# Linear attention stage of a three-stage kernel: norm gain and bias folded into the weights, the key minimum as the exponential's bias, an fp32 query product, and keys times values split by sequence

## The reference

```
x  = x + attention(ln(x)*(1+scale1)+shift1) @ proj * gamma1
x  = x + gelu((ln(x)*(1+scale2)+shift2) @ fc1 + b1) @ fc2 * gamma2       (b2 inside)
xn = ln(x) * norm_g + norm_b
q, k, v = xn @ Wq + bq, xn @ Wk + bk, xn @ Wv + bv        16 heads of 16
q  = softmax over the 16 channels of a head
k  = softmax over the 64 tokens of a sequence
ctx = k^T v by head;  y = q ctx
h  = silu(ln(y)*sn_g*(1+scale) + (sn_b*(1+scale) + shift)) @ out_W + out_b
x  = x + cond * h
```

## Time and profile before

| | us |
|---|---|
| median of 3 runs | 1348.47 |
| profiled execution | 1349.81 |
| its span | 1347.9 |
| busy PE, DVE, ACT, POOL | 1152.5, 994.8, 867.3, 933.9 |

### The profile page before, as it was taken

The page is one execution under the profiler, slowest core; times in us unless marked ns, Lnnn a source line. Parts: engine busy times, 40 slices in busy tenths (PEclk is TensorE's granted clock), DMA queues, the critical chain, the costliest instruction groups (busy, mean ns, idle before and its releaser), DMA issues. The chain is left out here.

```text
span 1347.9 us, 38178 instructions
## 1 busy us (share of the span) xinstructions
PE 1152.5 (86%) x12189; PEld 856.6 (64%) x12342; DVE 994.8 (74%) x2388; ACT 867.3 (64%) x2268; POOL 933.9 (69%) x1091
## 2 busy tenths in 40 slices
PE   2568898998989874899999999978888888888886
PEld 1356777777777763466666666655666666666664
DVE  2857787887878754745556465439999999999993
ACT  1456677777777762545454544528888888888884
POOL 3547677777777755656575765635788888888888
PEclk9789999999999997899999999989999999999997
DMA  5454233232333332110101001000011111111112
GB/s 149 152 112 117 56 52 62 54 60 56 57 61 53 65 54 66 40 32 16 32 16 31 18 29 32 17 16 7 24 37 51 35 35 50 36 37 36 52 36 71
DMA packets 142704, 67.73 MB, mean 50 GB/s; under 512 B 80688, under 2 KB 141360, under 8 KB 142640
## 3 DMA queue, kind: packets, MB, share of 16 engines
q1 hardware_dynamic: 109472, 40.53, 14.2%
q10 hardware_dynamic: 33168, 26.38, 6.9%
HBM read 41.18 MB, written 8.65 MB: 37 GB/s over the span
## 5 line engine op out<-in xcount | busy, mean ns | idle before, releaser
L1107 PE MATMUL f_ps_y<-w_fc,f_h_split 128*128 128x256 bf16 x1536 | 172.7, 273 | 1.4 <-DVE f_branch L1213 1.4
L1134 PE MATMUL f_ps_h<-f_x_split,w_fc 128*128 128x512 bf16 x737 | 165.8, 381 | 3.1 <-DVE f_x_split L1187 1.5
L1107 PEld LDWEIGHTS f_ps_y<-w_fc,f_h_split 128*128 128x128 bf16 x1536 | 150.2, 98 | 22.5 <-issue 1.7
L627 POOL TENSOR_TENSOR e_split<-e_full,e_split 128x1024 bf16<-128x1024 f32 x64 | 136.6, 2135 | 32.7 <-ACT e_full L700 31.6
L1221 DVE TENSOR_TENSOR f_h_split<-f_h,f_h_split 128x512 bf16<-128x512 f32 x64 | 65.0, 1018 | 103.0 <-ACT f_h L1091 103.0
L1090 ACT ACTIVATE f_h_split<-f_ps_h,b_fc 128x512 bf16<-128x512 f32 x128 | 89.0, 695 | 66.0 <-POOL f_h_split L1045 32.6
L1134 PEld LDWEIGHTS f_ps_h<-f_x_split,w_fc 128*128 128x128 bf16 x768 | 75.4, 98 | 87.0 <-issue 2.2
L609 POOL TENSOR_TENSOR x_split<-x_t,x_split 128x256 bf16<-128x256 f32 x64 | 44.6, 697 | 104.4 <-ACT x_split L649 104.4
L760 PE MATMUL ps_s<-qk_t,k_pairs 128*128 128x64 bf16 x3072 | 101.7, 194 | 11.7 <-DMA k_pairs<-qk_t 9.8
L760 PEld LDWEIGHTS ps_s<-qk_t,k_pairs 128*128 128x128 bf16 x3072 | 99.0, 99 | 14.5 <-DMA k_pairs<-qk_t 11.0
L1045 POOL TENSOR_TENSOR f_h_split<-f_h,f_h_split 128x512 bf16<-128x512 f32 x64 | 80.6, 1269 | 36.3 <-ACT f_h L1091 36.3
(11 more groups left out here) (171 smaller groups left out, 3416.1 us busy)
## 6 DMA issues: line engine op xcount, KB each, us to landing
v_pairs<-v_split SPq DMA_DIRECT2D x128, 66.0 KB, 2.1
k_pairs<-qk_t SPq DMA_DIRECT2D x256, 32.0 KB, 2.2
gain<-gammas SPq DMA_DIRECT2D x64, 128.0 KB, 3.0
f_gain<-gammas ACTq DMA_DIRECT2D x32, 256.0 KB, 4.3
l_gate<-in_cond ACTq DMA_DIRECT2D x128, 64.0 KB, 2.6
out<-x_all ACTq DMA_DIRECT2D x16, 512.0 KB, 2.9
x_all<-in_x SPq DMA_DIRECT2D x13, 512.0 KB, 6.5
w_ada<-in_L_cond_ada_w SPq DMA_DIRECT2D x1, 1536.0 KB, 8.3
```

The costliest lines, as they stand in the source:

```text
L627: pool.tensor_tensor(flat(e_split[a][:, LO]), flat(e_full[:]), flat(e_split[a][:, HI]), ALU.subtract).then_inc(e_lo_made, 1)
L1107: last = pe.matmul(ps_y[:, i], h_split[a][:, hs, f, i * P:(i + 1) * P], m.w_fc2[:, ws, f], start=(f == 0 and k == 0), stop=(f == F_CHUNKS ...
L1134: last = pe.matmul(ps_h[f % 4][:], m.w_fc1[:, ws, c, f * P:(f + 1) * P], x2_split[a][:, xs, c], start=(k == 0 and c == 0), stop=(k == 2 an ...
```

## The change

In the linear pass:

- The affine (L1480) is gone. norm_g is multiplied into the weights when they are split, norm_b times the weights is added to the biases. x3_high and x3_low read the transposed x from PSUM.
- The keys' weights and bias are negated. The minimum of the negated keys (with their bias in PSUM, two more matmuls in qkv) is used as bias of an exponential with scale -1. k_top_bias and k_shifts are gone.
- kq_high is split into k_high (bf16) and q_copy (fp32); kq_low becomes k_low, for the keys alone. kv_high and kv_low are gone, and q_kv is four fp32 matmuls in place of twelve in bf16.
- k_v becomes k_v_first, ahead of turn_kq and turn_x, and k_v_second, behind them. x3_high and x3_low come first in their steps.

In setup, the loads of bq, bv and bk and their part of the bias splitting are gone. In the feed-forward pass, SP loads the three biases behind the weights; DVE widens norm_b in step 0 (widen_norm3, first in its list); in step 5 PE makes four fp32 matmuls of norm_b with the weights and waits for DVE's two adds (carry_norm3, carry_biases3), DVE splits the sums into bf16 rows, and ACT and DVE make the split weights (split_qvk3), which ACT and POOL did at the end of the pass.

```diff
@@ feed_forward_pass
+            for k, source in enumerate((bq, bv, bk)):
+                sp.dma_start(biases3[:, k * C:(k + 1) * C], source[None, :].to_broadcast([P, C])).then_inc(qvk3_here, 16)
...
-                if isinstance(t.n, int) and t.n == BLOCKS - 1:
-                    pool.wait_ge(qvk3_hi_made, 1)
-                    pool.tensor_tensor(m.w_qvk3[:, LO], qvk3_full, m.w_qvk3[:, HI], ALU.subtract)
...
+            def carry_norm3(t):
+                if isinstance(t.n, int) and t.n == 2:
+                    pe.wait_ge(qvk3_here, 16 * 6)
+                    pe.wait_ge(norm3_widened, 2)
+                    pe.wait_ge(h_made, t.n * F_CHUNKS)
+                    for bank, cols in ((0, slice(0, 2 * C)), (1, slice(2 * C, 3 * C))):
+                        for c in range(NC_):
+                            last = pe.matmul(ps_h[bank][:, 0:cols.stop - cols.start], b_norm3_wide[:, c],
+                                             qvk3_full[:, c, cols], start=(c == 0), stop=(c == NC_ - 1))
+                    last.then_inc(norm3_carried, 1)
+                    pe.wait_ge(biases3_summed, 2)
-            run(pe, [(3, fc1_first), (4, fc2_first), (3, fc1_second), (1, turn_x), (4, fc2_second)])
+            run(pe, [(3, carry_norm3), (3, fc1_first), (4, fc2_first), (3, fc1_second), (1, turn_x), (4, fc2_second)])
...
+            def widen_norm3(t):
+                if isinstance(t.n, int) and t.n == 0:
+                    dve.wait_ge(m.linear_here, 16 * 3)
+                    dve.tensor_copy(b_norm3_wide, m.b_norm3[:, :, None].to_broadcast([P, NC_, P])
+                                    ).then_inc(norm3_widened, 1)
+                    dve.tensor_scalar(minus_g_norm3[:], m.g_norm3[:], -1.0, None, ALU.mult).then_inc(norm3_widened, 1)
+            def split_qvk3(t):
+                if isinstance(t.n, int) and t.n == 2:
+                    dve.wait_ge(qvk3_hi_made, 2 * NC_)
+                    for c in range(NC_):
+                        for cols, g in ((slice(0, 2 * C), m.g_norm3), (slice(2 * C, 3 * C), minus_g_norm3)):
+                            dve.scalar_tensor_tensor(m.w_qvk3[:, LO, c, cols], qvk3_full[:, c, cols], g[:, c:c + 1],
+                                                     m.w_qvk3[:, HI, c, cols], ALU.mult, ALU.subtract)
-            run(dve, [(2, scale), (1, hat), (-1, statistics), (0, aggregate), (2, x2_low), (3, h_low_even),
-                      (4, residual), (4, last_residual)])
+            run(dve, [(0, widen_norm3), (3, carry_biases3), (2, scale), (1, hat), (-1, statistics), (0, aggregate), (2, x2_low), (3, h_low_even),
+                      (3, split_qvk3), (4, residual), (4, last_residual)])
@@ linear_pass
-                        q_cols = C + c * P + s * L
-                        for i, (q, w) in enumerate(SPLITS):
-                            last = pe.matmul(ps_y[s * L:(s + 1) * L, c * P:(c + 1) * P],
-                                             kq_t[t.slot(4)][:, q, q_cols:q_cols + L], kv_split[a][:, w, c, s],
-                                             start=(i == 0), stop=(i == 2))
+                        q_cols = c * P + s * L
+                        last = pe.matmul(ps_y[s * L:(s + 1) * L, c * P:(c + 1) * P],
+                                         q_t[t.slot(4)][:, q_cols:q_cols + L], kv[a][:, c, s], start=True, stop=True)
...
+                    pe.matmul(ps_k[:, to], m.rows_k3[:, to * P:(to + 1) * P], m.ones[:], start=True, stop=False)
...
-            pipeline(pe, [(6, k_v), (5, turn_kq), (0, turn_x), (11, project), (2, qkv), (7, q_kv),
+            pipeline(pe, [(6, k_v_first), (5, turn_kq), (0, turn_x), (6, k_v_second), (11, project), (2, qkv), (7, q_kv),
                           (Y_LAG, turn_y)])
...
-            pipeline(act, [(3, v_high), (1, affine), (9, load_gate), (1, x3_high), (5, kq_high),
-                           (3, k_exponentials), (9, modulate), (3, q_exponentials), (6, kv_high), (13, store),
+            pipeline(act, [(1, x3_high), (3, v_high), (9, load_gate), (5, k_high), (5, q_copy),
+                           (3, k_exponentials), (9, modulate), (3, q_exponentials), (13, store),
                            (9, tanhs)])
...
-            pipeline(dve, [(-2, statistics), (3, k_maxima), (Y_LAG, y_statistics), (3, q_maxima), (3, k_top_bias),
-                           (-1, aggregate), (3, q_lower), (3, v_low), (3, k_shifts), (Y_LAG, y_aggregate),
-                           (6, mask), (5, kq_low), (-1, hat), (4, total), (Y_LAG, y_hats), (1, x3_low),
+            pipeline(dve, [(-2, statistics), (1, x3_low), (3, k_maxima), (Y_LAG, y_statistics), (3, q_maxima),
+                           (-1, aggregate), (3, q_lower), (3, v_low), (Y_LAG, y_aggregate),
+                           (6, mask), (5, k_low), (-1, hat), (4, total), (Y_LAG, y_hats),
                            (11, residual)])
```

More of the change, by code:

```diff
@@ L248, in _ @@
             load(act, [(head_scale[:], scale_mul.rearrange("a h b c -> (a b c) h").to_broadcast([P, H]))], heads_here)
-            load(act, [(bias_full[:, i * C:(i + 1) * C], row(b)) for i, b in enumerate((v_bias, proj_b, bq, bv, out_b))],
+            load(act, [(bias_full[:, i * C:(i + 1) * C], row(b)) for i, b in enumerate((v_bias, proj_b, out_b))],
                  biases_here)
@@ L256, in _ @@
             load(act, [(m.b_fc1[:], column(fc1_b)), (m.b_fc2[:], row(fc2_b))], m.ff_here)
-            load(act, [(m.b_k3[:], column(bk)), (m.g_norm3[:], column(norm_g)), (m.b_norm3[:], column(norm_b))],
-                 m.linear_here)
+            load(act, [(m.g_norm3[:], column(norm_g)), (m.b_norm3[:], column(norm_b))], m.linear_here)
             act.wait_ge(heads_made, 1)
@@ L1046, in h_low_odd @@
                                        ).then_inc(h_lo_odd, 1)
-            run(pool, [(2, shift), (2, split_fc2), (0, rstd_of), (5, update), (5, add), (3, h_low_odd),
-                       (3, split_qvk3)])
+            run(pool, [(2, shift), (2, split_fc2), (0, rstd_of), (5, update), (5, add), (3, h_low_odd)])
         @block.scalar
@@ L1253, in linear_pass @@
         k_tops = sb("k_tops", [P, NC_, SEQ])
-        k_shift = sb("k_shift", [P, NC_, SEQ])
         q_tops = sb("q_tops", [P, H])
@@ L1403, in power @@
                                    ).then_inc(rstd_made, 1)
-            pipeline(pool, [(5, softmax), (7, kv_low), (-1, inverse_deviations), (Y_LAG, last_inverse_deviations),
+            pipeline(pool, [(5, softmax), (-1, inverse_deviations), (Y_LAG, last_inverse_deviations),
                             (10, silus), (12, add)])
@@ L1464, in k_exponentials @@
                         act.activation(kq[t.slot(4)][:, i * L:(i + 1) * L], ps_k[:, c, s * L:(s + 1) * L], ACT.Exp,
-                                       bias=k_shift[a][:, c, s:s + 1], accum_out=sums[t.slot(4)][:, i:i + 1]
+                                       bias=k_tops[a][:, c, s:s + 1], scale=-1.0, accum_out=sums[t.slot(4)][:, i:i + 1]
                                        ).then_inc(k_exp_made, 1)
@@ L1568, in qkv @@
                             last = pe.matmul(ps_k[:, to], m.w_qvk3[:, ws, c, cols], x3_split[a][:, xs, c],
-                                             start=(i == 0 and c == 0), stop=(i == 2 and c == NC_ - 1))
+                                             start=False, stop=(i == 2 and c == NC_ - 1))
                 last.then_inc(k_done, 1)
@@ L1618, in mask, with k_low @@
                                   ).then_inc(kv_masked, 1)
[L1620 to L1623 removed]
+            def k_low(t):
+                dve.wait_ge(q_t_made, t.n + 1)
+                dve.wait_ge(k_hi_made, t.n + 1)
+                dve.tensor_tensor(k_t[t.slot(4)][:, LO], ps_kq[:, 0:C], k_t[t.slot(4)][:, HI], ALU.subtract
+                                  ).then_inc(k_lo_made, 1)
             def total(t):
```

175 lines of the change are left out of this document (86 added, 89 removed).

## The result

The changed kernel takes 1331.4 us (median of 4 runs, 1328.7 to 1332.7) against 1347.95 for the kernel before (4 runs, 1347.26 to 1349.31): ratio 0.9873, 95% interval 0.9855 to 0.9891. That is 16.6 us less where the forecast had 7.

What follows compares the result with a forecast made beforehand. TensorE was to replace VectorE as bound, at 6.45 us a step; setup -2.5, feed-forward +5.4 +4.1 +0.5, filling -4, steady steps -8, draining -3 sum to -7.5: 1342.3 profiled, 1341 median. Range 1327 to 1354.

Steps and rivals of the forecast that it cites:

- I take 0.96, so +0.36: Linear stage, TensorE: q_kv as eight fp32 records takes 0.96 us a step instead of 0.60.
- The cycle through the mask: Linear stage: loop binding TensorE and VectorE, from q_kv through mask, hat, sums and y_hat back, 6.1 us in all.
- VectorE's 1.09: Linear stage: VectorE loses 0.54 + 0.07 + 0.27 + 0.21 us a step, making its step 5.5.
- Keys times values split, about 0: Linear stage, TensorE: 0.24 wait saved, 0.13 + 0.1 paid for a second shape change; bounds -0.24 and +0.15.
- Filling, -4 with bounds 0 and -11: First 10 steps of the linear stage: VectorE nearly full, 0.4 us a step gained, -4.
- Feed-forward start +5.4, fold +4.1 and residual +0.5: Feed-forward stage: widen_norm3 waits for w_out's load, +5.4; step 5's bias folding holds TensorE, +4.1; late residual, +0.5.
- Setup -2.5: Setup: two broadcasts fewer at 1 us each, and b_k's load of 0.46 gone; bounds -0.5 and -4.
- Draining -3: End of the linear stage: 4 steps without kv_low, -4.4; 3 steps set by TensorE, +1.5; bounds -6 and +1.5.
- Rival A: Linear stage: fp32 query product cheap (halves overlap, +0.15), 0.25 to 0.3 a step more gained, 1327 us; chance 0.13.
- B: Linear stage: fp32 query product at 0.15 us a record, TensorE's step 6.8, 1358 us; chance 0.14.
- C: Linear stage: cycle through the mask decides, y_hats after TensorE is ready, step 6.6, 1349 us; chance 0.20.
- D: Linear stage: VectorE alone sets 5.5 us a step, 1296 us; chance 0.01.

Runs made afterwards that it cites:

- q_full: Changed kernel with 128 columns of query weights in each fp32 query matmul instead of 64 (first sequence's result wrong); 1341.5 us.
- no_k_bias: Changed kernel with four split-x buffers, widen_norm3 in step 1, norm_b fold in the feed-forward stage's last step, and no key biases; 1310.0 us.
- q32_pool: Kernel before with the fp32 query product alone, but GpSimd's kv_low kept, its result unread; 1348.2 us.
- kv_together: Changed kernel with both sequences' products of keys and values one behind the other ahead of the transposes, as in the kernel before; 1336.2 us.
- x3_slots4: Changed kernel with four buffers for the split x (x3_split) in place of two; 1324.1 us.
- setup_loads: Changed kernel with two 128 KB broadcast loads put back on ACT's setup queue, into a buffer nobody reads; 1333.6 us.
- q_alternate: Changed kernel with the four fp32 query matmuls reordered so that the two column halves alternate at each matmul; 1333.3 us.

## Why the prediction was too small

- **"I take 0.96, so +0.36"** for q_kv is the step that failed. It measured 0.59 to 0.60, +0.00. The price came from L326, whose weights have 128 columns; these have 64. q_full shows 0.95 for 128 in this very place. The error is 0.36 x 50 = 18 us of the 19.6 by which the steady steps were missed; the rest is the 0.03 for loop registers, which came to nothing measurable. What was left of TensorE's sum stood: 5.95 + 0.11 + 0 = 6.06, and 6.06 was measured. Luck is in the total: the steady steps were 19.6 too slow in the forecast and the filling 11.6 too fast, and only because the two offset each other does the time lie in the range and 10 us off.
- **TensorE takes VectorE's place as the bound:** right (99.9 against 94.6 us of 100; no_k_bias). The cycle through the mask was put at 6.1; it is at most the 5.94 of no_k_bias. With 0.60 in place of 0.96 for q_kv the same sum gives 5.7.
- **VectorE's 1.09:** too much, and VectorE was to be busy 85 to 90%. By its busy share (99.4% of 6.61, 94.6% of 6.06) it went from 6.57 to 5.73 a step, 0.84 less; which term fell short was not tested. kq_low's 0.27 was worth next to nothing in q32_pool, where x_hat waited instead. Of the bias add's 0.54, 0.46 was the stand behind kv_low.
- **Keys times values split, about 0:** right (+0.02 a step, kv_together).
- **Filling, -4 with bounds 0 and -11:** wrong in sign, +7.6. I priced the operations that go and not the wait that the new order brings: x3_high for the key product of two tiles before, with VectorE's whole list behind x3_low. This was readable from the lists. It hid 7.5 us of the gain (x3_slots4), some 3 of them by way of TensorE's clock.
- **Feed-forward start +5.4, fold +4.1 and residual +0.5:** mechanisms right; +4.8, and +5.7 for the last two: 2.75 + 1.19 on TensorE for the fold (forecast 4.1), 0.87 for the residual (0.5), the rest not traced.
- **Setup -2.5:** right mechanism, too small; -4.8, of which two loads are 2.9 (setup_loads), about 1.5 each instead of 1.
- **Draining -3:** -4.9. TensorE's share (+1.5) rested on the same 0.96, but the clock differs between the two executions, so this row proves nothing.
- **Rival A** had nearly the time (1327, step 6.1 to 6.2) and the cheap product, by a mechanism that q_alternate excludes. B, C and D did not come; with C, its sign did not (TensorE waits for l_y_hat 3 times).

The attention pass, which the change doesn't touch, scatters besides. In some profiles the draining is 3 to 4 us longer than after's, and there TensorE's granted clock is at the lower of its two levels (1.2 and 2.4 GHz) for some 10 us, as here in x3_slots4 (the means of two stretches are 0.88 and 0.61), after TensorE had been busy 10 us of 10. What decides this is not known.

```profile
1285.00:1295.00 10.00, 8.41 (x69) 5.78 (x66) 6.53 (x19) 6.40 (x25) 7.89 (x14) 0.88 0.08 26
1295.00:1305.00 10.00, 9.76 (x58) 6.38 (x58) 4.63 (x13) 3.89 (x12) 5.23 (x10) 0.61 0.26 79
```
